# Layer 0 of a two-layer attention kernel: joining the group statistics' pieces in four written-out iterations

## What is computed

```python
def _gn(v, G=32, eps=1e-5):
    g = v.reshape(B_, H_, W_, G, C_ // G)
    m = jnp.mean(g, axis=(1, 2, 4), keepdims=True)
    s = jnp.var(g, axis=(1, 2, 4), keepdims=True)
    return ((g - m) / jnp.sqrt(s + eps)).reshape(v.shape)

x = x + _L0_conv_ref(_gn(x), ...)   # 4 heads of 64, one softmax attention per image row
x = x + _L1_conv_ref(_gn(x), ...)   # 8 heads of 32, one softmax attention per channel
```

## Time and profile before

| | us |
|---|---|
| median of 3 runs | 4951.82 (4950.63 to 4952.84) |
| the profiled execution, device time | 4953.47 |
| its span, first to last instruction | 4951.5 |
| busy: TensorE / VectorE / ScalarE / GpSimd | 4653.2 / 4023.9 / 3527.3 / 3466.7 |
| stages in the span: first pass and before / gs0 and the start of layer 0 / layer 0 in its stride / seam / layer 1 | 0 to 423 / 423 to 500 / 500 to 2880 / 2880 to 2930 / 2930 to 4951 |

### The profile page before, as it was taken

The page is one execution under the profiler, slowest core; times in us unless marked ns, Lnnn a source line. Parts: engine busy times, 40 slices in busy tenths (PEclk is TensorE's granted clock), DMA queues, the critical chain, the costliest instruction groups (busy, mean ns, idle before and its releaser), DMA issues. The chain is left out here.

```text
span 4951.5 us, 149914 instructions
## 1 busy us (share of the span) xinstructions
PE 4653.2 (94%) x44087; PEld 3924.4 (79%) x44087; DVE 4023.9 (81%) x12779; ACT 3527.3 (71%) x11216; POOL 3466.7 (70%) x5926
## 2 busy tenths in 40 slices
PE   4663999999999999999999969999999999999999
PEld 2332888888888888888888858888888888888887
DVE  4445888888888888888888878888888888888887
ACT  2222888888888888888888846666666666666665
POOL 2332888888888888888888826666666666666665
PEclk8776999999999999999999979999999999999999
DMA  8995111111111111111111101111111111111111
GB/s 331 354 350 176 53 51 59 59 51 59 55 55 59 51 59 59 51 59 56 54 59 51 53 26 53 48 49 49 51 51 51 51 51 51 51 51 51 51 50 39
DMA packets 237329, 382.52 MB, mean 77 GB/s; under 512 B 18756, under 2 KB 156616, under 8 KB 224968
## 3 DMA queue, kind: packets, MB, share of 16 engines
q1 hardware_dynamic: 237256, 381.63, 23.0%
HBM read 309.21 MB, written 72.35 MB: 77 GB/s over the span
## 5 line engine op out<-in xcount | busy, mean ns | idle before, releaser
L1302 POOL TENSOR_SCALAR l_probs<-l_probs,l_inv 128x256 f32<-128x256 f32 x2048 | 944.3, 479 | 737.1 <-DVE l_inv L1207 731.7
L1126 ACT ACTIVATE l_probs<-bank,l_neg_max 128x256 f32<-128x256 f32 x2048 | 949.1, 482 | 486.2 <-DVE l_neg_max L1201 486.2
L545 POOL TENSOR_SCALAR l_probs<-l_probs,l_inv 128x256 f32<-128x256 f32 x2048 | 949.4, 479 | 269.0 <-DVE l_inv L796 269.0
L714 ACT ACTIVATE l_probs<-l_probs,l_neg_max 128x256 f32<-128x256 f32 x2048 | 1020.0, 518 | 1.5 <-DVE l_neg_max L788 1.3
L788 DVE CUSTOM_DVE_ANT_0 l_probs<-bank,bias 128x256 f32<-128x256 f32 x2048 | 779.8, 418 | 219.8 <-PE bank L655 215.6
L1201 DVE TENSOR_REDUCE l_neg_max<-bank 128x2 f32<-128x512 f32 x1024 | 646.7, 683 | 92.6 <-PE bank L1035 92.6
L1214 DVE TENSOR_TENSOR l_probs_t<-bank,bias 128x512 f32<-128x512 f32 x1024 | 674.1, 681 | 37.7 <-PE bank L1045 22.6
L655 PE MATMUL bank<-ident,l_probs 128*128 128x128 f32 x4096 | 629.4, 276 | 1.0 <-POOL l_probs L545 0.6
L1045 PE MATMUL bank<-ident,l_probs 128*128 128x128 f32 x4096 | 532.4, 273 | 3.1 <-DVE l_probs_t L1214 1.7
L668 PE MATMUL bank<-l_probs_t,l_v 128*64 128x256 f32 x4096 | 498.5, 385 | 0.7 <-DVE l_probs_t L810 0.5
L655 PEld LDWEIGHTS bank<-ident,l_probs 128*128 128x128 f32 x4096 | 463.9, 141 | 36.7 <-POOL l_probs L545 1.7
(11 more groups left out here) (193 smaller groups left out, 14002.8 us busy)
## 6 DMA issues: line engine op xcount, KB each, us to landing
fp_x<-in_x_dram SPq DMA_DIRECT2D x32, 1024.0 KB, 6.9
fp_ln_w<-in_L_conv_ln_w_dram SPq DMA_DIRECT2D x32, 1024.0 KB, 8.9
fp_ln_b<-in_L_conv_ln_b_dram SPq DMA_DIRECT2D x32, 1024.0 KB, 10.2
fp_pair<-in_L_conv_pair_repr_dram SPq DMA_DIRECT2D x32, 1024.0 KB, 12.1
l_x<-in_x_dram SPq DMA_DIRECT2D x128, 256.0 KB, 2.9
l_ln_w<-in_L_conv_ln_w_dram SPq DMA_DIRECT2D x128, 256.0 KB, 3.3
l_ln_b<-in_L_conv_ln_b_dram SPq DMA_DIRECT2D x128, 256.0 KB, 3.5
x<-l_y SPq DMA_DIRECT2D x128, 256.0 KB, 2.0
```

The source lines that it names most:

```text
L545: last = nc.gpsimd.tensor_scalar(probs[:, h, c], probs[:, h, c], inv[:, h, c:c + 1], 1.0, ALU.mult, ALU.mult)
L714: last = nc.scalar.activation(probs[:, h, c], probs[:, h, c], ACT.Exp, bias=neg_max[:, h, c:c + 1], scale=-1.0, accum_out=total[:, h, c:c ...
L1126: last = nc.scalar.activation(probs[:, h, c], b_s[h % 4][:, c * W:(c + 1) * W], ACT.Exp, bias=neg_max[:, h, c:c + 1], accum_out=total[:, h ...
L1302: last = nc.gpsimd.tensor_scalar(probs[:, h, c], probs[:, h, c], inv[:, h, c:c + 1], 1.0, ALU.mult, ALU.mult)
```

## The change

- `layer0`'s VectorE rows no longer run in one loop of 30 passes but through `loop_stops_peeled`: iterations 0, 8, 15, 22, 29 and 31 are written out, and between them stand five loops of 7, 6, 6, 6 and 1 passes. The other engines keep their loop.
- In the written-out iterations t = 8, 15, 22 and 29 a new `join(t, k)` follows `measure` at each step k: a wait for the measurement of the step before, and one `bn_aggr` for each of four groups over the pieces t - 7 to t - 1 (42 values). Its mean and variance go behind a count of 448 (7 pieces of 64 elements) that stands there already, so that they form one triple.
- Behind the loops two `tensor_scalar` multiply the variances of the joined triples by 448 (28 groups by 4 and 4 groups by 4 values).
- The pieces of the first iteration go to slot 32 in place of 0, the left-over pieces to slot 33; two or three more slots hold the joined triples and the counts. `prepare_weights` gets one `memset` of 576 values per partition for the counts.
- gs1's 32 `bn_aggr` read slots 29 to 35 (42 values) for g < 28, and 29 to 34 (36 values) for the others. gs0's are unchanged.

```diff
--- before.py
+++ after.py
@@ -51,14 +51,29 @@
     body(count - 1, False, True)
 
 
-def over_rows(engine, total, unroll, row, ahead=3, behind=1, hinted=None):
+def loop_stops_peeled(engine, count, stops, body, hinted):
+
+
+    body(0, True, False)
+    done = 1
+    for stop in (*stops, count - 1):
+        with hinted.Fori(done, stop, engines=[engine.engine], hint_back_edge=True) as t:
+            body(t, False, False)
+        body(stop, False, stop == count - 1)
+        done = stop + 1
+
+
+def over_rows(engine, total, unroll, row, ahead=3, behind=1, hinted=None, stops=None):
 
 
 
     def body(t, first, last):
         for k in range(-ahead if first else 0, unroll + behind if last else unroll):
             row(t, k, lambda d, k=k: (not first or k + d >= 0) and (not last or k + d < unroll))
-    loop_ends_peeled(engine, total // unroll, body, hinted)
+    if stops:
+        loop_stops_peeled(engine, total // unroll, stops, body, hinted)
+    else:
+        loop_ends_peeled(engine, total // unroll, body, hinted)
 
 
 class Chain:
@@ -82,7 +97,7 @@
     return nc.tensor.matmul(out, ll, rh, start=False, stop=stop)
 
 
-def prepare_weights(nc, m, a, load_first_tiles):
+def prepare_weights(nc, m, a, stats, load_first_tiles):
 
 
     with ExitStack() as ctx:
@@ -138,6 +153,7 @@
             nc.vector.memset(wb[:], 0.0)
             nc.vector.memset(m.w_pair[:], 0.0).then_inc(zeroed, 1)
             nc.vector.memset(m.averager[:], 1.0 / P)
+            nc.vector.memset(stats[:, :, W // 8 + 1:W // 8 + 4, :], 7.0 * 8 * GROUP)
             dve.wait_ge(loaded, 16 * LOADS)
 
             nc.vector.tensor_copy(wrep_h[:], wrep[:].rearrange("o c h -> o h c")).then_inc(permuted, 1)
@@ -342,7 +358,7 @@
             loop_first_peeled(pool, TILES // 2, body)
 
 
-def finish_statistics(nc, m, tag, stats, chunks, with_layer_norm, biases=None, turn_bias=False):
+def finish_statistics(nc, m, tag, pieces, with_layer_norm, biases=None, turn_bias=False):
 
 
 
@@ -383,7 +399,7 @@
         @block.vector
         def _(dve):
             for g in range(NG):
-                last = nc.vector.bn_aggr(own[:, g, :], stats[:, g, 0:chunks(g), :])
+                last = nc.vector.bn_aggr(own[:, g, :], pieces(g))
             last.then_inc(own_ready, 1)
             chain = Chain(dve, step)
             dve.wait_ge(own_ready, 1)
@@ -462,6 +478,8 @@
     UNROLL, TILE = 8, 2
     BUFS = UNROLL // TILE
     AHEAD = 5
+    ITERATIONS = W // UNROLL
+    JOINED, PER_JOIN = (7, 14, 21, 28), 7
     PAIRS = NH0 // 2
     with ExitStack() as ctx:
         sem = lambda name: ctx.enter_context(nc.semaphore(f"l0_{name}"))
@@ -501,8 +519,8 @@
             "o_ready", "o_high", "o_split", "out_mm", "y_ready", "measured"))
         block = ctx.enter_context(nc.Block())
 
-        def rows(engine, row, hinted=None):
-            over_rows(engine, W, UNROLL, row, ahead=AHEAD, behind=1, hinted=hinted)
+        def rows(engine, row, hinted=None, stops=None):
+            over_rows(engine, W, UNROLL, row, ahead=AHEAD, behind=1, hinted=hinted, stops=stops)
 
         @block.sync
         def _(sp):
@@ -842,10 +860,22 @@
                 for g in range(NG // UNROLL * kk, NG // UNROLL * (kk + 1)):
                     columns = slice(g * GROUP, (g + 1) * GROUP)
                     if isinstance(tt, int) and tt == 0:
-                        last = nc.vector.bn_stats(stats[:, g, 0, :], y[:, 0:kk + 1, columns])
+                        last = nc.vector.bn_stats(stats[:, g, ITERATIONS, :], y[:, 0:kk + 1, columns])
                     else:
                         last = nc.vector.bn_stats(stats[:, g, tt, :], y[:, :, columns])
                 last.then_inc(measured, 1)
+
+            def joined_at(g):
+                return ITERATIONS + 1 if g >= NG - NG // UNROLL else ITERATIONS + 2
+
+            def join(t, k):
+
+                if isinstance(t, int) and t - 1 in JOINED:
+                    s = JOINED.index(t - 1)
+                    dve.wait_ge(measured, UNROLL * t + k)
+                    for g in range(NG // UNROLL * k, NG // UNROLL * (k + 1)):
+                        nc.vector.bn_aggr(stats[:, g, joined_at(g) + s // 2, 3 * (s % 2) + 1:3 * (s % 2) + 3],
+                                          stats[:, g, t - PER_JOIN:t, :])
 
             def row(t, k, has):
                 if has(0):
@@ -876,9 +906,14 @@
                     inverse(t, k + 2, 2)
                 if has(0):
                     measure(t, k)
-            rows(dve, row, hinted=nc)
+                    join(t, k)
+            rows(dve, row, hinted=nc, stops=[last + 1 for last in JOINED])
+            for groups in (slice(0, NG - NG // UNROLL), slice(NG - NG // UNROLL, NG)):
+                at = joined_at(groups.start)
+                spreads = stats[:, groups, at:at + 2, :].rearrange("p g s (e v) -> p g (s e) v", v=3)[:, :, :, 2]
+                nc.vector.tensor_scalar(spreads, spreads, float(PER_JOIN * UNROLL * GROUP), None, ALU.mult)
             for g in range(NG - NG // UNROLL):
-                nc.vector.bn_stats(stats[:, g, W // UNROLL, :], y[:, g // (NG // UNROLL) + 1:UNROLL, g * GROUP:(g + 1) * GROUP])
+                nc.vector.bn_stats(stats[:, g, ITERATIONS + 1, :], y[:, g // (NG // UNROLL) + 1:UNROLL, g * GROUP:(g + 1) * GROUP])
 
 
 def layer1(nc, m, x1, out):
@@ -1353,7 +1388,7 @@
         m.bias1 = sb("bias1", [P, KC, NH1, W])
         m.mean = sb("mean", [P, W])
         m.rstd = sb("rstd", [P, W])
-        stats = sb("chunk_stats", [P, NG, W // 8 + 1, 6])
+        stats = sb("chunk_stats", [P, NG, W // 8 + 4, 6])
         image_parts = nc.dram_tensor("image_bias_parts", (3, NH0, W, W), F32).ap()
         pair_bias = nc.dram_tensor("pair_bias", (NH1, W, W), F32).ap()
         x1 = nc.dram_tensor("x1", (C0, W, W), F32).ap()
@@ -1367,12 +1402,12 @@
                 for i in range(2):
                     image.load(sp, i, i)
 
-            prepare_weights(nc, m, args, load_first_tiles)
+            prepare_weights(nc, m, args, stats, load_first_tiles)
             first_pass(nc, m, image, pair_repr, image_parts, pair_bias, stats)
-        finish_statistics(nc, m, "gs0", stats, lambda g: W // 8, True, (image_parts, pair_bias))
+        finish_statistics(nc, m, "gs0", lambda g: stats[:, g, 0:W // 8, :], True, (image_parts, pair_bias))
         layer0(nc, m, x, ln_w, ln_b, x1, stats)
 
-        finish_statistics(nc, m, "gs1", stats, lambda g: W // 8 + (g < NG - 4), False, turn_bias=True)
+        finish_statistics(nc, m, "gs1", lambda g: stats[:, g, 29:36 - (g >= NG - 4), :], False, turn_bias=True)
         layer1(nc, m, x1, out)
 
 
```

## The result

| | before | after |
|---|---|---|
| device time, median of 8 runs each, us | 4951.93 (4946.78 to 4952.87) | 4937.62 (4934.86 to 4940.88) |
| ratio, with its 95% interval | | 0.9973 (0.9965 to 0.9982) |
| profiled execution: time / span, us | 4953.47 / 4951.53 | 4934.87 / 4932.89 |
| to gs0's first `bn_aggr`, us | 423.35 | 421.31 |
| from there to gs1's first `bn_aggr` (layer 0), us | 2461.17 | 2471.18 |

The kernel is 14.3 us faster, where the forecast was 20.1. The four lower lines add up to the spans. The seam gives back 22.5 us, layer 0 takes 10.0 us more, and the profiled execution is 6.1 us shorter in two stretches that hold none of the change's work but the one `memset` at the start (it was also, to 0.01 us, the shortest of its eight).

The account below looks back on a forecast made before the run. TensorE bounds at large, VectorE's 32 `bn_aggr` the seam between layers. Terms -22.6 + 0.2 + 0 + 0 + 2.3 = -20.1 us, from 4951.8 to 4931.7 us; range 4925.5 to 4940, the forecast's own 4928 to 4936.

Parts of the forecast that it names:

- The seam: Between layer 0 and layer 1, where 32 `bn_aggr` take 29.07 us on VectorE and TensorE waits 24.11 us.
- What bounded: TensorE at large, but VectorE's 32 `bn_aggr` between the layers; a microsecond off them is one off the time.
- Part 1: gs1's `bn_aggr` between the layers, over 42 or 36 values: 6.5 us for all 32, 22.6 us less.
- neighbour's fixed part: Other end for gs1's `bn_aggr`: 0.055 us fixed, taken from `bn_stats`, giving 7.6 us in all, 21.5 less.
- Part 2: Two products before the left-over `bn_stats` cost 0.2 us; the `memset` at the start, in VectorE's idle time, nothing.
- Part 3: Joins in 32 written-out rows of layer 0, 0.82 us of VectorE each: cost 0, at most 4 us.
- rival (c): Joined rows in layer 0 don't fit: 0.3 us a row shows at TensorE, 9.6 us, 4941; one in twelve.
- Part 4: Five loops for one in layer 0: four more exits at 0.56 us, 2.3 us more, between 0 and 5.9.
- (b): Loop exits and entries in layer 0 stall dearer, each of four at 1.48 us: 7 us, 4937; 15 in 100.
- loop of one pass: Item in (b): layer 0's loop of a single pass was to cost one stall more.
- The rule on instruction fetch: Skill's rule for layer 0's loops: 21 jumps back cost, falls through don't; by it alone the sum is 2.3 us lower.
- Rival (a), the clock,: TensorE's clock between the layers doesn't fall, or comes back sooner: up to 6 us less, 4925.7; a tenth.

Follow-up runs that it names:

- short `bn_aggr` alone: Kernel before, with gs1's `bn_aggr` reading only seven or six pieces and the others left out: 4927.31 us against 4951.08, ratio 0.995.
- joins at the end: Changed kernel with one loop over iterations 1 to 27 and the joins in written-out iterations 28 to 31: 4931.55 us against 4953.23, ratio 0.9957.
- changed, 38 memsets: Changed kernel with 38 one-value `memset` at the start that only move VectorE's later code: 4928.43 us against 4951.59, ratio 0.9952.
- before, 10 memsets: Kernel before with ten one-value `memset` at the start that only move VectorE's later code, no joins: 4947.91 us, one run.

## Why the prediction was right and wrong

**What bounded: right.** The seam was VectorE's, nothing else was late behind it, and 29.07 - 6.53 = 22.5 us came off (23.8 in the runs of the short `bn_aggr` alone).

**Part 1, 6.5 us for gs1: right.** 28 of 42 and four of 36 values take 6.53 us, so the line through two sizes of the instruction itself held down to a fifth of them, and the 7.6 us from a neighbour's fixed part was too much. The Trainium skill's 58 + n cycles (VectorE: DVE Perf Modes, the TRN2 errata) would have said an estimated 3.3 us for 32 of them; the trace does not agree.

**Part 2, products and `memset`: right.** 0.20 us; 0.54 us at 1.25 us, in front of an idle time of 8.82 us.

**Part 3, the joins at 0: right.** A joined row has 9.34 us, so rival (c) did not come. The cover was narrower than forecast: at double the joins the row takes 9.65, so that beyond the single joins 0.81 - 0.31 = 0.5 us were free, where the prediction had 0.07 in the row and another 0.76 of tolerance.

**Part 4, four exits at 0.56 us: wrong.** The step that failed is "Four more such exits" at 4 x 0.56 = 2.3 us, with 4 x 1.48 = 5.9 as its upper end. It measured 9.4 us: four stalls of 3 us, 2.07 to 2.11 us each, and 3.71 for the last. Three things were wrong in it. The 1.48 us was taken for the size of the stall, where it is what shows of a longer one; the upper bound was therefore none. The 0.56 was taken for its cost, though it is a difference: what shows, less about 0.9 us that the row absorbs (in front of the copies 1.48 costs 0.56, 2.15 costs 1.20, 2.97 costs 2.07, and 0.81 nothing). And one case was taken four times, as if the place of the stall in the row were given. It moves with the length of the code; in the change the length brought all four to the same bad place, and in the run without the joins to four different ones, which cost 2.0 us more than before. That the forecast's 2.3 fits this run is luck, since two of its four stalls cost nothing and two over 1.2 us. Whether a join makes a stall dearer stays open: the plain stall at that copy was 2.15 us, the joined ones 2.97 and more.

The measured time lies inside the range of 4925.5 to 4940, near its upper end, and outside the forecast's own, 4928 to 4936. With 9.4 in place of 2.3 the sum is -22.6 + 0.2 + 9.4 = -13.0 us; measured was -14.3, and the interval (0.9965 to 0.9982, 9 to 17 us) holds both. Of the rivals it was (b) that came, with 7.1 us more of exits than forecast where it had about 5. That its time, 4937, is the measured one is in part luck: its price of 1.48 an exit is too low, and its "loop of one pass" doesn't exist as a cost (0.37 us of stall, nothing lost).

**The rule on instruction fetch.** The prediction priced straight code behind an exit against the Trainium skill (Runtime: NRT & Kernel Launch, Instruction fetch mechanics), which has the stalls at taken branches. Without the hint the trace agrees with the page: each of the 21 jumps costs 1.7 to 1.8 us and the exits nothing. With the hint it does not agree: the jumps cost nothing and the exits do. The prediction was right to price the exits; by the rule alone their term would have been 0, where 9.4 us were measured.

**Rival (a), the clock,** came in part. Before, TensorE's granted clock was low (1.2 GHz) from 2880.4 us for 6.8 us and from 2894.1 for 47.8; after, from 2888.4 for 10.2, from 2902.0 for 20.5, and once more for 3.4. In the profiled execution the stretch behind the `bn_aggr` is 4.1 us shorter. But among all thirteen traces that stretch lies between 2031.8 and 2038.0 us, in kernels with the long seam (2031.9, 2034.7) as well as with the short one (2037.7), and the time to gs0 lies between 419.6 and 425.9. So it is not shown that the change earned it.

## What to carry to other kernels

Work that was moved out of this seam into idle time in the loop was nearly free, as long as it fitted (0.81 us a row did, twice that did not); what it cost is the code that carries it there. If that means more exits of a hinted loop on an engine with long unrolled bodies, look in the trace for the stall without a releaser behind an exit and price it by the worst place (here 3.1 us of stall and up to 3.7 us of time), not by what one lucky place shows; then place the written-out code so that it falls in front of work that can wait. Joins behind a single exit, with a plain iteration in between, came out 25.9 us under the kernel before in place of 14.3, and the change itself with its code moved by 38 instructions 23.2.

## What the runs showed of the hardware

- **The load behind an exit.** The trace's record of DMA packets has one of 8192 bytes on instruction queue q14 shortly before every stall behind an exit but one (the 0.37 us one). VectorE goes on 1.72 to 1.88 us after its start, in all 23 stalls read in eleven kernels; six of them:

```
kernel                     packet at   VectorE goes on   stall
before                     2840.04     2841.85           1.48
after, first               1118.46     1120.19           2.97
after, fourth              2694.00     2695.74           3.14
joins at the end           2615.99     2617.72           3.24
changed, 38 memsets        1113.59     1115.31           1.39
before, 10 memsets         2834.52     2836.32           2.15
```

  In the change each hinted loop has such packets in its first pass (two behind the first joined iteration, at 1195.23 and 1220.03) and none from there to the exit (the next is at 1643.56). Its first joined iteration begins behind the exit at 1095.96; the packet comes 22.5 us later, and the stall stands in front of the 105th recorded instruction. With the 38 `memset` the packet comes 14.5 us after the exit.
- **A stall costs less than its length.** Of a stall of 1.4 to 3.0 us in front of one of the copies these rows absorb 0.9 to 1.0 us (1.48 us cost 0.56, 2.97 cost 2.07); elsewhere in the row it was 0.6 to 1.3 us.
- **One stand of TensorE can cost twice.** It stood 1.77 us behind the first stall, and its granted clock stayed at 1.00 (2.4 GHz). With every join twice it stood 1.87 us at one place, and the clock stayed too. It stood 1.95 us behind the fourth, and 2.05 in the version with its joins at the end, and the clock went to 1.2 GHz for 3.4 us, which made that stall 1.6 us dearer (3.71 for 2.1).
- **`bn_aggr` is nearly all slope.** 4.5 ns a value from 198 down to 42 values, 0.205 us for one of 42 (read off groups of 32 in 29.07 and 6.53 us).
